# Two waits of TensorE set to earlier counts: the second FFN matmul of superblock 0, and the staging of attention

## The chip, the cores and the metric

The kernel runs on the 8 cores of one Trainium2 chip. Each core holds one of the 8 batch elements and runs the same program; the cores exchange nothing. The metric is the device time in microseconds (us) of the slowest core.

## What is computed

One macaron layer on `x` of shape 8 x 2048 x 1024: half an FFN, attention, half an FFN, each on a LayerNorm of `x`.

```python
x = x + 0.5 * ffn(layernorm(x))
x = x + attn(layernorm(x))
x = x + 0.5 * ffn(layernorm(x))

def ffn(x):   # D = 1024, hidden 4096; two routed experts, one shared
    top1 = argmax(softmax(x @ gate_w.T))
    masked = x[None] * one_hot(top1, 2).T[:, :, None]
    h = relu(einsum('end,edh->enh', masked, w1) + b1[:, None])
    routed = (einsum('enh,ehd->end', h, w2) + b2[:, None]).sum(0)
    return routed + relu(x @ sw1 + sb1) @ sw2 + sb2

def attn(x):  # 16 heads of 64, a plain reshape; q = k = v
    q = x @ wq.T + bq
    qh = q.reshape(16, b, s, 64)
    a = softmax(qh @ qh.T / 32)
    return (a @ qh).reshape(b, s, 1024) @ wu.T + bu
```

## The kernel before

`x` stays in SBUF for the whole kernel (`x_sb`, features on the partitions, 2048 tokens along the free side). The program is written out by hand through a small recorder, `Sched`: `emit` appends an instruction to one engine's list, `bump` raises the recorded count of a semaphore (DVE for VectorE, ACTs for ScalarE, MM for TensorE), and `wait` makes an engine wait until a semaphore has reached a count, unless it has already waited for as much. Each engine runs its list in order, so every wait holds whatever stands behind it on its engine.

**FFN** (`emit_ffn`, run twice). The tokens form four strips of 512. The hidden side of all three experts is cut into 12 superblocks of 1024. For each superblock and strip, `do_mm1` makes the hidden tile in 8 groups of 8 matmuls, into ps_a and ps_b in turn (L556), with ScalarE's Relu after each (L566); `do_mm2` makes the output in 8 groups `dc` of 8 matmuls, into ps_c and ps_d in turn (L593). VectorE adds each group onto `x_sb` (L606 in superblock 0, L613 in the others), and only then is its bank free for the group after next (`ps2_free`). In superblock 0 the LayerNorm is woven in. `sf[st]` makes the sums of a strip (L326, L353). `pf[st]` makes the scale and the mean (TensorE's broadcasts at L391 and L402 among it) and then the normalized strip, in 16 VectorE instructions (L411, L415, eight times each). `gf[st]` makes the gate and masks. The order of superblock 0 is, for each strip: `do_mm1(st)`, `sf[st + 2]`, `pf[st + 1]`, `do_mm2(st)`, where the first two exist for strips up to 1 and 2.

**Attention** (`emit_attn`). 2048 rows are handled in 16 blocks `i` of 128 rows, and each block has 16 rows of tiles `a`. `qproj(half)` makes q for eight blocks, ahead of block 0 and of block 8. `staging(i)` copies a block's q from `q_ap` into `ar_h`, doubled over the partitions, in four groups `b4` of four matmuls (L690) into `stg[b4 % 2]`, which are s0 and s1; VectorE casts each group out (L700). `transposes(i)` follows (L713, cast at L724). `sc_row(i, a)` makes four score matmuls (L742) with ScalarE's exponential after each (L753). Score matmuls go to s0 and s1 in turn, and from `a` = 4 on also to ps_t. `av_row(i, a)` multiplies the exponentials with q, four matmuls (L770). Within a block the order on TensorE is: score rows 0 to 2; AV rows 3 to 15 of the block before; transposes; score rows 3 to 15, with the tail of the block before in between (its sums, L837, L846, and its output projection, L868, L881); AV rows 0 to 2; `staging(i + 1)`. In blocks 0 and 8 the staging and the transposes come straight after `qproj` instead.

The names that the change touches: `xwait_dve` is the VectorE count that the FFN was given as the point from which `x_sb` is complete (0 for the first FFN, attention's last addition for the second). `sch.val(DVE)` is the VectorE count of everything recorded so far. `state["stage_ev"]` and `act_prev` hold the count of the last staging cast; `state["stage_tok"][i]` is what `transposes` and `sc_row` wait for.

Of the kernel before, what the change touches and what calls it, by code (L numbers as in the profile page):

```python
# [29 lines left out]
def c_of_pos(p):  # L30
    return 2 * p if p < 8 else 2 * (p - 8) + 1
# [37 lines left out]
def build(phases=("ffn1", "attn", "ffn2")):  # L69
# [15 lines left out]
    with es:  # L85
# [40 lines left out]
        sch = Sched()  # L126
        X, MM, ACTs, DVE, GP, OUT = "x", "mm", "act", "dve", "gp", "out"
# [14 lines left out]
        def q_ap(kc, t0, w):  # L142
            return ar_b[:, kc * 1024 + t0: kc * 1024 + t0 + w]
# [18 lines left out]
        def w2blk(slot, hc, dc):  # L162
            o = slot * 8192 + hc * 1024 + dc * 128
            return ar_w2[:, o:o + 128]
# [335 lines left out]
        def emit_ffn(xwait_dve, wst, ps_d, ps_w, ps_w2, ps_e, ps_f):  # L500
# [81 lines left out]
            def do_mm2(sup, st, slot, mm2_extra):  # L582
                h_all = max(h_relu_tok)
                for dc in range(NKC):
                    pst = (ps_c, ps_d)[dc % 2]
                    sch.wait("tensor", DVE, max(ps2_free[dc % 2], mm2_extra))
                    if dc > 0:
                        sch.wait("tensor", ACTs, h_all)
                    for hc in range(NKC):
                        if dc == 0:  # L590
                            sch.wait("tensor", ACTs, h_relu_tok[hc])
                        def f2(t, S, _hc=hc, _dc=dc, _slot=slot, _pst=pst):
                            ins = t.matmul(_pst[:, :], w2blk(_slot, _hc, _dc),  # L593
                                           ar_h[:, _hc * TS:(_hc + 1) * TS],
                                           start=(_hc == 0), stop=(_hc == NKC - 1))
                            if _hc == NKC - 1:
                                ins.then_inc(S[MM], 1)
                        sch.emit("tensor", f2)
                    g2 = sch.bump(MM, 1)
                    sch.wait("vector", MM, g2)  # L600
                    sch.wait("vector", DVE, tok_b2)
                    o0 = dc * NT + st * TS
                    if sup == 0:
                        def fx(v, S, _dc=dc, _o0=o0, _pst=pst):
                            xsl = x_sb[:, _o0:_o0 + TS]
                            v.scalar_tensor_tensor(  # L606
                                out=xsl, in0=_pst[:, :],
                                scalar=b2sh[:, _dc:_dc + 1], in1=xsl,
                                op0=ALU.add, op1=ALU.add).then_inc(S[DVE], 1)
                    else:  # L610
                        def fx(v, S, _o0=o0, _pst=pst):
                            xsl = x_sb[:, _o0:_o0 + TS]
                            v.tensor_add(xsl, xsl, _pst[:, :]).then_inc(S[DVE], 1)  # L613
                    sch.emit("vector", fx)
                    stt_tok[dc][st] = sch.bump(DVE, 1)
                    ps2_free[dc % 2] = stt_tok[dc][st]
                    if pending_lnm:
                        pending_lnm.pop(0)()
                while pending_lnm:
                    pending_lnm.pop(0)()  # L620

            sf[0](); sf[1](); pf[0]()
            for st in range(NSTRIP):
                do_mm1(0, st, 0, 0)
                if st + 2 < NSTRIP:
                    sf[st + 2]()
                if st + 1 < NSTRIP:
                    pf[st + 1]()
                do_mm2(0, st, 0, sch.val(DVE))
                if st == 2:  # L630
                    ext["all_ln"] = max(ln_tok)
                if st >= 2:
                    gf[st - 2]()
# [20 lines left out]
        def emit_attn(xwait_dve, s0, s1, d_att, ps_t, ps_rz, hooks):  # L654
# [9 lines left out]
            state = {  # L664
                "exp_tok": {},
                "avtok": {},
                "avfree": 0,
                "stage_tok": {},
                "stage_ev": 0,
                "ufree": 0,  # L670
                "qT_tok": {},
                "zsum_tok": 0,
# [5 lines left out]

            def staging(i, q_ready):
                qoff = (i % 8) * 128  # L680
                act_prev = state["stage_ev"]
                for b4 in range(4):
                    ps = stg[b4 % 2]
                    sch.wait("tensor", ACTs, state["sreg_last"].get(b4 % 2, 0))
                    sch.wait("tensor", DVE, max(q_ready, act_prev))
                    for j in range(4):
                        c = c_of_pos(b4 * 4 + j)
                        hb = (c % 2) * 64
                        def fqq(t, S, _c=c, _hb=hb, _q=qoff, _j=j, _ps=ps):
                            ins = t.matmul(_ps[:, _j * 128:(_j + 1) * 128],  # L690
                                           e2mat[_hb:_hb + 64, :],
                                           q_ap(_c // 2, _q, 128)[_hb:_hb + 64, :],
                                           start=(_j == 0), stop=(_j == 3))
                            if _j == 3:
                                ins.then_inc(S[MM], 1)
                        sch.emit("tensor", fqq)
                    gqq = sch.bump(MM, 1)
                    sch.wait("vector", MM, gqq)
                    def fqqe(v, S, _b4=b4, _ps=ps):
                        v.tensor_copy(ar_h[:, _b4 * TS:(_b4 + 1) * TS],  # L700
                                      _ps[:, :]).then_inc(S[DVE], 1)
                    sch.emit("vector", fqqe)
                    act_prev = sch.bump(DVE, 1)
                state["stage_ev"] = act_prev
                state["stage_tok"][i] = act_prev

            def transposes(i):
                sch.wait("tensor", DVE, state["stage_tok"][i])
# [187 lines left out]
            def qproj(half):  # L896
                t0h = half * 1024
                qev = [0, 0]
                for dc in range(NKC):
                    for st2 in range(2):  # L900
                        t0 = t0h + st2 * TS
                        pst = stg_u[(dc * 2 + st2) % 2]
                        sch.wait("tensor", *wready["wq"])
                        sch.wait("tensor", DVE, max(ln_tok[half * 2 + st2],
                                                    state["avfree"],
                                                    state["ufree"]))
                        sch.wait("tensor", DVE, qev[(dc * 2 + st2) % 2])
                        for kc in range(NKC):
                            def fq(t, S, _kc=kc, _dc=dc, _t0=t0, _pst=pst):
                                ins = t.matmul(_pst[:, :], wqtblk(_kc, _dc),  # L910
                                               ln_ap(_kc, _t0, TS),
                                               start=(_kc == 0), stop=(_kc == NKC - 1))
                                if _kc == NKC - 1:
                                    ins.then_inc(S[MM], 1)
                            sch.emit("tensor", fq)
                        gq = sch.bump(MM, 1)
                        sch.wait("vector", MM, gq)
                        def fqe(v, S, _dc=dc, _toff=t0 - t0h, _pst=pst):
                            v.tensor_scalar_add(q_ap(_dc, _toff, TS), _pst[:, :],
                                                bq_sb[:, _dc:_dc + 1]).then_inc(S[DVE], 1)  # L920
                        sch.emit("vector", fqe)
                        qev[(dc * 2 + st2) % 2] = sch.bump(DVE, 1)
                return max(qev)

            q_ready = qproj(0)
            if "after_qproj0" in hooks:
                hooks["after_qproj0"](sch.val(MM))
            staging(0, q_ready)
            transposes(0)
            for i in range(16):  # L930
                if i == 8:
# [4 lines left out]
                    q_ready = qproj(1)  # L936
# [197 lines left out]
```

## Time and profile before

| | us |
|---|---|
| median of 3 runs | 4235.93 (4235.05 to 4821.63) |
| the profiled execution, own time | 4235.93 |
| its span, slowest core | 4234.3 |
| TensorE busy (matmuls) | 3814.1 |
| ScalarE busy | 1221.5 |
| VectorE busy | 1137.0 |

The span runs from the first to the last instruction of the slowest core, and the execution's own time lies 1.6 us around it. PE stands for TensorE's matmuls, PEld for its weight loads, DVE for VectorE, ACT for ScalarE. A row of a timeline gives the start and the duration in us, and in brackets how long the engine had been idle and what released it. Matmuls are pipelined: a row of 8 starts 8 times, and the next row may start before it ends. PEclk in a row of stretches is the granted clock of TensorE, as a share of its full 2.4 GHz; it takes the two values 0.50 and 1.00, and what lies between is a mean.

### The profile page before, as it was taken

How to read it: one execution, taken by the hardware profiler on the slowest of the kernel's cores; microseconds unless marked ns; L12 is line 12 of the kernel's file. 1: busy time of each engine (PE TensorE's matmuls, PEld its weight loads, DVE VectorE, ACT ScalarE, POOL GpSimd, SP SyncE). 2: the span in 40 equal slices, each digit the busy share in tenths (PEclk: the TensorE clock that was granted, in tenths of full speed). 3: DMA queues.
4: the chain of work that ended last, by engine and by line, in shares of the span. 5: the costliest groups of instructions: out<-in, count | busy, mean ns of one | idle time of the engine just before them, and what ended most of it. 6: DMA issues, size and time to landing. Idle time of an engine off the chain costs nothing. (4 is left out here: it accounts for less than half of the span.)

```text
span 4234.3 us, 45694 instructions; the slowest of 8 cores (4229.7 to 4234.3 us)
## 1 busy us (share of the span) xinstructions
PE 3814.1 (90%) x16880; PEld 1593.2 (38%) x16880; DVE 1137.0 (27%) x2179; ACT 1221.5 (29%) x2956; POOL 48.5 (1%) x67
## 2 busy tenths in 40 slices
PE   3679999999999996888888888867999999999998
PEld 0234444444444431233332333322344444444443
DVE  1332212333222325121231212233222222333222
ACT  1111122111222121765637656421111122111221
POOL 0000000000000000000000000000000000000000
PEclk8799999999999997566575665778999999999999
DMA  7002222222222100100001000210222222222202
GB/s 159 0 1 40 40 40 40 40 40 40 40 40 40 20 1 1 20 1 1 1 1 21 1 1 1 42 18 0 40 40 40 40 40 40 40 40 40 32 10 80
DMA packets 55268, 124.63 MB, mean 29 GB/s; under 512 B 1808, under 2 KB 1808, under 8 KB 53008
## 3 DMA queue, kind: packets, MB, share of 16 engines
q0 software_dynamic: 52144, 104.86, 16.0%
q1 hardware_dynamic: 2912, 16.85, 1.2%
q8 instruction: 144, 2.36, 0.2%
q14 instruction: 68, 0.56, 0.0%
HBM read 218.18 MB, written 8.39 MB: 54 GB/s over the span
## 5 line engine op out<-in xcount | busy, mean ns | idle before, releaser
L566 ACT ACTIVATE ar_h<-ps_a,b1hf 128x512 bf16<-128x512 f32 x384 | 263.9, 687 | 1914.6 <-PE ps_a L556 1914.6
L593 PE MATMUL ps_c<-ar_h,ar_w 128*128 128x512 bf16 x3072 | 735.8, 383 | 78.3 <-DVE ar_ln L415 78.3
L593 PE MATMUL ps_d<-ar_h,ar_w 128*128 128x512 bf16 x3072 | 729.2, 380 | 0.0
L613 DVE TENSOR_TENSOR x_sb<-x_sb,ps_c 128x512 f32<-128x512 f32 x352 | 241.9, 687 | 1501.3 <-PE ps_c L593 1501.3
L556 PE MATMUL ps_a<-ar_b,ar_w 128*128 128x512 bf16 x2048 | 485.8, 379 | 2.8 <-DVE ar_b L522 2.6
L556 PE MATMUL ps_b<-ar_b,ar_w 128*128 128x512 bf16 x2048 | 483.8, 379 | 0.0
L742 PE MATMUL s<-ar_h 64*128 64x512 bf16 x768 | 413.8, 565 | 74.0 <-ACT ar_w L753 53.1
L593 PEld LDWEIGHTS ps_c<-ar_h,ar_w 128*128 128x128 bf16 x3072 | 302.2, 99 | 452.7 <-issue 96.0
L593 PEld LDWEIGHTS ps_d<-ar_h,ar_w 128*128 128x128 bf16 x3072 | 302.0, 98 | 366.8 <-issue 7.8
L566 ACT ACTIVATE ar_h<-ps_b,b1hf 128x512 bf16<-128x512 f32 x384 | 263.9, 687 | 402.5 <-PE ps_b L556 402.5
L753 ACT ACTIVATE ar_w<-s 128x512 bf16<-128x512 f32 x432 | 255.3, 600 | 335.7 <-PE s L742 334.9
L613 DVE TENSOR_TENSOR x_sb<-x_sb,ps_d 128x512 f32<-128x512 f32 x352 | 241.9, 687 | 283.3 <-PE ps_d L593 283.3
L556 PEld LDWEIGHTS ps_a<-ar_b,ar_w 128*128 128x128 bf16 x2048 | 200.1, 98 | 254.4 <-issue 21.8
L556 PEld LDWEIGHTS ps_b<-ar_b,ar_w 128*128 128x128 bf16 x2048 | 200.2, 98 | 234.7
L556 PE MATMUL ps_a<-ar_ln,ar_w 128*128 128x512 bf16 x1024 | 252.0, 387 | 17.8 <-DVE ar_ln L415 17.8
L556 PE MATMUL ps_b<-ar_ln,ar_w 128*128 128x512 bf16 x1024 | 247.5, 385 | 0.0
L522 DVE TENSOR_TENSOR ar_b<-ar_ln,ar_b 128x512 bf16<-128x512 bf16 x512 | 212.9, 418 | 0.0
L742 PEld LDWEIGHTS s<-ar_h 64*128 64x128 bf16 x768 | 75.0, 103 | 361.8 <-issue 360.7
L556 PEld LDWEIGHTS ps_a<-ar_ln,ar_w 128*128 128x128 bf16 x1024 | 101.0, 99 | 151.4 <-issue 35.9
L742 PE MATMUL ps_t<-ar_h 64*128 64x512 bf16 x256 | 147.7, 577 | 5.3 <-ACT p_ex L753 0.4
L556 PEld LDWEIGHTS ps_b<-ar_ln,ar_w 128*128 128x128 bf16 x1024 | 101.7, 99 | 125.1 <-issue 7.8
L753 ACT ACTIVATE ar_ln<-s 128x512 bf16<-128x512 f32 x176 | 105.4, 615 | 43.6 <-PE s L742 43.6
(162 smaller groups left out, 2466.6 us busy)
## 6 DMA issues: line engine op xcount, KB each, us to landing
ar_w<-w1c POOLq DMA_DIRECT2D x24, 2048.0 KB, 18.3
ar_w<-w2c POOLq DMA_DIRECT2D x24, 2048.0 KB, 28.9
x_sb<-x SPq DMA_DIRECT2D x1, 8192.0 KB, 37.3
y<-x_sb SPq DMA_DIRECT2D x8, 1024.0 KB, 10.7
ar_w<-wqt POOLq DMA_DIRECT2D x1, 2048.0 KB, 17.3
ar_w<-wut POOLq DMA_DIRECT2D x1, 2048.0 KB, 16.7
b1hf<-b1h SPq DMA_DIRECT2D x1, 48.0 KB, 38.8
bq_sb<-bqc SPq DMA_DIRECT2D x1, 4.0 KB, 40.1
```

What stands on the lines that cost most here:

```text
L522: v.tensor_mul(lnm_ap(_kc), ln_ap(_kc, _st * TS, TS), mask_ap(_w, _st)).then_inc(S[DVE], 1)
L556: ins = t.matmul(_pst[:, :], w1blk(_slot, _kc, _hc), _rhs(_kc), start=(_kc == 0), stop=(_kc == NKC - 1))
L566: s.activation(ar_h[:, _hc * TS:(_hc + 1) * TS], _pst[:, :], AF.Relu, bias=b1hf[:, _sup * 8 + _hc:_sup * 8 + _hc + 1], scale=0.5).then_inc ...
L593: ins = t.matmul(_pst[:, :], w2blk(_slot, _hc, _dc), ar_h[:, _hc * TS:(_hc + 1) * TS], start=(_hc == 0), stop=(_hc == NKC - 1))
L613: v.tensor_add(xsl, xsl, _pst[:, :]).then_inc(S[DVE], 1)
L742: t.matmul(_sr[:, :], qq_ap(_pa, _h), ar_h[_h:_h + 64, _q4 * TS:(_q4 + 1) * TS], start=True, stop=True).then_inc(S[MM], 1)
L753: s.activation(prow_ap(_a)[:, _q4 * TS:(_q4 + 1) * TS], _sr[:, :], AF.Exp, scale=SCALE, accum_out=_z[:, _a * 4 + _q4:_a * 4 + _q4 + 1]).th ...
```

## The change

Two places are changed, both of them only in what TensorE waits for.

In superblock 0 of each FFN, `do_mm2` gets `xwait_dve` as its extra VectorE count instead of `sch.val(DVE)`. The waits on the bank (`ps2_free`) and on the Relu outputs stay.

In `staging`, one count for the last cast (`stage_ev`, `act_prev`) becomes one count for each of the two banks (`stage_ev2`). A group of staging matmuls waits for the last cast of its own bank instead of the last cast of either. The count that the readers of the staged data wait for is still that of the last cast.

```diff
@@ -626,7 +626,7 @@
                 if st + 1 < NSTRIP:
                     pf[st + 1]()
-                do_mm2(0, st, 0, sch.val(DVE))
+                do_mm2(0, st, 0, xwait_dve)
@@ -666,7 +666,7 @@
-                "stage_ev": 0,
+                "stage_ev2": [0, 0],
@@ -678,11 +678,11 @@
             def staging(i, q_ready):
                 qoff = (i % 8) * 128
-                act_prev = state["stage_ev"]
                 for b4 in range(4):
                     ps = stg[b4 % 2]
                     sch.wait("tensor", ACTs, state["sreg_last"].get(b4 % 2, 0))
-                    sch.wait("tensor", DVE, max(q_ready, act_prev))
+                    sch.wait("tensor", DVE,
+                             max(q_ready, state["stage_ev2"][b4 % 2]))
@@ -700,9 +700,8 @@
                     sch.emit("vector", fqqe)
-                    act_prev = sch.bump(DVE, 1)
-                state["stage_ev"] = act_prev
-                state["stage_tok"][i] = act_prev
+                    state["stage_ev2"][b4 % 2] = sch.bump(DVE, 1)
+                state["stage_tok"][i] = max(state["stage_ev2"])
```

## Rows read from the trace of the kernel before

**Rows 1.** The page: head, part 1, and the TensorE clock of part 2 (tenths, 40 slices).
```profile
span 4234.3 us, 45694 instructions; the slowest of 8 cores (4229.7 to 4234.3 us)
...
PE 3814.1 (90%) x16880; PEld 1593.2 (38%) x16880; DVE 1137.0 (27%) x2179; ACT 1221.5 (29%) x2956; POOL 48.5 (1%) x67
...
PEclk8799999999999997566575665778999999999999
```

**Rows 2.** Waits of TensorE: line <- releaser: us in total, times, longest.
```profile
PE ps_c L593 <- DVE ar_ln L415: 78.3, 6, 13.3
...
PE s L690 <- DVE ar_h L700: 46.7, 48, 1.3
```

**Rows 3.** Timeline, strip 0 of the second FFN: start, us, engine [idle before <-releaser].
```profile
2798.87 0.69 DVE L411 TENSOR_TENSOR ar_ln<-x_sb,ps_f 128x512 bf16<-128x512 f32 x1 [6.03 <-PE ps_f L402]
...
2810.77 0.69 DVE L415 TENSOR_TENSOR ar_ln<-ar_ln,p_ex 128x512 bf16<-128x512 bf16 x1
...
2811.61 3.57 PE L593 MATMUL ps_c<-ar_h,ar_w 128*128 128x512 bf16 x8 [12.98 <-DVE ar_ln L415]
...
2815.30 0.75 DVE L606 SCALAR_TENSOR_TENSOR x_sb<-ps_c,b2sh,x_sb 128x512 f32<-128x512 f32 x1 [3.84 <-PE ps_c L593]
...
2817.40 1.89 PE L593 MATMUL ps_c<-ar_h,ar_w 128*128 128x512 bf16 x8
...
2819.13 1.89 PE L593 MATMUL ps_d<-ar_h,ar_w 128*128 128x512 bf16 x8
```

**Rows 4.** Stretch: busy us of PE, PEld, DVE, ACT, POOL, then PEclk, DMA.
```profile
2811.61:2816.38 4.77, 4.77 (x12) 1.75 (x13) 0.75 (x1) 0.00 (x0) 0.00 (x0) 0.50 0.00 0
```

**Rows 5.** Timeline of one staging, matmuls and casts, to the first score matmuls.
```profile
1802.14 0.60 PE L690 MATMUL s<-ar_b,e2mat 64*128 64x128 bf16 x4
1802.85 0.69 DVE L700 CAST ar_h<-s 128x512 bf16<-128x512 f32 x1 [11.87 <-PE s L690]
...
1803.69 0.38 PE L690 MATMUL s<-ar_b,e2mat 64*128 64x128 bf16 x4 [0.94 <-DVE ar_h L700]
1804.17 0.69 DVE L700 CAST ar_h<-s 128x512 bf16<-128x512 f32 x1 [0.63 <-PE s L690]
...
1807.02 0.69 DVE L700 CAST ar_h<-s 128x512 bf16<-128x512 f32 x1 [0.83 <-PE s L690]
...
1807.86 1.01 PE L742 MATMUL s<-ar_h 64*128 64x512 bf16 x2 [0.94 <-DVE ar_h L700]
```

**Rows 6.** Stretches: three intervals between stagings, then three stagings.
```profile
1738.58:1802.14 63.56, 55.61 (x244) 20.46 (x242) 13.25 (x36) 39.05 (x129) 0.00 (x0) 0.55 0.00 1
1864.16:1925.65 61.49, 53.07 (x244) 19.58 (x242) 13.25 (x36) 38.84 (x129) 0.00 (x0) 0.61 0.00 1
1925.65:1987.00 61.35, 53.30 (x244) 19.64 (x242) 13.25 (x36) 38.84 (x129) 0.00 (x0) 0.61 0.00 1
1738.58:1745.05 6.47, 2.35 (x19) 1.40 (x18) 2.76 (x4) 0.00 (x0) 0.00 (x0) 0.50 0.00 1
...
1864.16:1870.04 5.88, 1.74 (x18) 1.06 (x17) 2.77 (x4) 0.00 (x0) 0.00 (x0) 0.78 0.01 1
1925.65:1931.16 5.51, 1.74 (x19) 1.06 (x18) 2.77 (x4) 0.00 (x0) 0.00 (x0) 0.80 0.00 0
```

**Rows 7.** Timeline of VectorE: two instructions in a row with no wait between.
```profile
1403.61 0.69 DVE L613 TENSOR_TENSOR x_sb<-x_sb,ps_c 128x512 f32<-128x512 f32 x1 [14.52 <-PE ps_c L593]
1404.21 0.42 DVE L522 TENSOR_TENSOR ar_b<-ar_ln,ar_b 128x512 bf16<-128x512 bf16 x1
```

**Rows 8.** Stretches at the AV matmuls of two blocks; the transposes that follow them.
```profile
1878.70:1881.13 2.43, 2.43 (x13) 1.09 (x14) 0.00 (x0) 0.84 (x4) 0.00 (x0) 0.50 0.00 0
1881.13:1891.37 10.24, 8.60 (x73) 3.74 (x69) 1.94 (x5) 4.88 (x17) 0.00 (x0) 1.00 0.00 0
1753.69:1758.25 4.56, 4.56 (x23) 2.02 (x24) 0.00 (x0) 0.86 (x4) 0.00 (x0) 0.50 0.02 4
...
1885.61 0.55 PE L713 MATMUL ps_t<-ident,ar_h 64*128 64x64 bf16 x13
```

## The prediction

> **What bounds the kernel now.** I read the page's head first: all eight cores lie within 4.6 us of each other, so one core stands for the chip. Then its parts 1 and 2: TensorE is busy 90% of the span and is the engine at its limit, and in the middle of the kernel, slices 16 to 26, which hold attention, the clock line of TensorE falls to 5 to 7 tenths of full speed [rows 1]. So a microsecond in which TensorE waits is, as a rule, a microsecond of the span. That leads to the third view, what TensorE waits for [rows 2]. Both edits aim at lines of it: 78.3 us in 6 waits of the second FFN matmul (L593) for the LayerNorm's last multiply (L415), and 46.7 us in 48 waits of the staging matmuls (L690) for their own casts (L700). Together they are 125 us, 3% of the span. How much of it goes is read from the timelines of one place of each kind.
>
> **Edit 1, the wait ahead of `do_mm2` in superblock 0.** The old argument, the VectorE count at the time of the call, holds the first w2 matmul until `pf[st + 1]` has finished all 16 of its VectorE instructions. The new one is a count reached long before. In the timeline those 16 run from 2798.87 to 2811.46 at a pitch of 0.79, and TensorE stands idle for 12.98 us [rows 3]. There are six such places: strips 0, 1 and 2 of both FFNs. Strip 3 calls no `pf`, and its count is met long before, since the view has only six waits of this kind.
>
> The wait does not vanish. The first two groups of eight matmuls (dc 0 and 1) have free banks and can run in the gap. Group 2 needs the bank of group 0 back, and the addition that frees it (L606) stands in VectorE's queue behind the same 16 instructions. So group 2 starts after the last multiply, plus 0.10 to the next VectorE instruction, plus 0.75 for the L606, plus 0.15 to TensorE: 0.85 later than group 0 starts today. Sixteen matmuls are out of the way by then. At full clock a group takes 1.73, the start spacing of later groups, so these are worth 3.45. Gain: 3.45 - 0.85 = 2.6 us.
>
> The clock does not change this much. Today the 16 matmuls run from 2811.61 to 2817.40, in 5.79 us, since the granted clock is 0.50 (the 1.2 GHz level) for the first 4.77 us after the idle stretch [rows 3, 4]. After the edit they run at that level inside the gap, about 6.8 us (16 at the 0.43 of today's cold ones), and TensorE is then idle again for some 7 us, so I expect groups 2 and 3 to pay the same 5.79 - 3.45 = 2.3 us. If the clock stays up over those 7 us, the gain is 2.6 + 2.3 = 4.9. VectorE's and ScalarE's work is unchanged. Nothing else waits behind the removed wait, and the next `do_mm1` follows at once and gives the gain on. Edit 1: 6 x 2.6 = **16 us**, with ends 6 x 2 = 12 (another 0.6 lost in each) and 6 x 4.9 = 29.
>
> **Edit 2, a token per bank in `staging`.** Four groups of four matmuls fill s0 and s1 in turn, and each group is cast by VectorE. Today each group waits for the cast just before it, which read the other bank. The timeline shows the serial chain: cast 0.69, 0.15 to TensorE, group, 0.48 from its start to the next cast, so 1.32 from cast to cast where the group takes 0.38, and some 1.55 where it takes 0.60 and the cast comes 0.71 after its start, as for the first group [rows 5]. From the first staging matmul to the first score matmul this takes 5.51 to 6.47 us [rows 6]; I take 5.6 over the 16 stagings. It is bare: ScalarE, with no exponentials left, shows 0.00 us of work in those stretches [rows 6], so it lies on the path.
>
> After the edit groups 0 and 1 run back to back, and the casts follow one another. VectorE can start an instruction 0.60 after the one before [rows 7]. Cast 2 waits for cast 0's end, 0.15, and 0.48 or 0.71 for the group, so it starts 1.32 to 1.55 after cast 0; cast 3 starts 0.60 to 0.75 after that, and ends 2.6 to 3.0 after cast 0's start. With 0.48 or 0.71 in front and 0.15 behind, the staging takes 3.3 to 3.85; I take 3.4, since most stagings have fast groups. Gain 5.6 - 3.4 = 2.2 us, times 16 = **35 us**. The bounds of each gain are 1.7 (slow groups in a short staging, 5.51 - 3.85) and 3.1. The copied data are the same, and the score rows wait for all four casts as before.
>
> **What is given back through the clock.** From one staging to the next takes about 61.5 us, of which the array has the full clock only for short stretches, 0.61 on the mean [rows 6]. The largest begins in the long run of AV matmuls (L770): these start, and the clock rises 2.43 us later, from 0.50 to 1.00, and stays up 10.24 us [rows 8]. In the first such block it rose 4.56 us after their start, 2.1 later; that interval is 63.56, 2.07 longer than the usual one, and its staging is 0.96 longer than the shortest, which leaves 1.1 us as the price of the late rise [rows 6, 8]. A matmul pair at half clock costs double, so a rise 1 us later costs 0.5.
>
> Further, the intervals hardly follow the staging: stagings of 5.88 and 5.51 stand in intervals of 61.49 and 61.35 [rows 6]. Of 0.37 us only 0.14 shows. So the clock's rises have their own spacing, and AV matmuls that start 2.2 us earlier may have to run longer at the low level. The rise at 2.43 us is the early end of these rows, so a shift costs more often than it gains. I take 0.8 of each 2.2 as lost in the 14 blocks whose staging is followed by another block: **11 us**, from 0 to 14 x 2.2 = 31.
>
> **Sum.** 16 + 35 - 11 = 40 us off the profiled execution, whose own time is 4235.93 around a span of 4234.3, and which is also the median of the runs shown: 4235.9 - 40 = **4196 us**.
>
> The Trainium skill, "TensorE: Matmul & The Clock Gate", section "HAM oscillation — how this bites in real kernels", reports a kernel in which PSUM double-buffering "gave no further gain". Edit 2 is double-buffering of PSUM. By that rule its term would be near 0 and the sum 4220, against 4196 by the rows here; this trace shows no double-buffered staging, so it can't yet say.
>
> **The rivals.**
> - *The clock moves along.* The rises follow the work, and edit 2 keeps all: 4235.9 - 16 - 35 = **4185**. For it: the stretches of full clock begin only in dense array work, which moves with the staging. Against: the 0.14 of 0.37 above.
> - *The staging gain is eaten.* The interval stays at some 61.4 because the AV matmuls wait for nothing but run longer at 1.2 GHz. Only the stagings of blocks 0 and 8 gain, which stand outside the repeating intervals: 2 x 2.2 = 4, less 1 for a clock edge. 4235.9 - 16 - 3 = **4217**. For it: the same 0.14 of 0.37, and the longer first interval. Against: a loss of 2.2 needs a rise 4.4 us later, and the latest seen is 2.1 later than the usual. (The rule named above would land beside this one.)
> - *The clock is better placed.* 47 of 61.5 us are at the low level, so a shift can also win. With the 4.9 in each place of edit 1 and nothing lost in edit 2: 4235.9 - 29 - 35 = **4172**.
> - *Slower: the long high stretch is lost.* If the AV run no longer brought the clock up, its bare part, from 1881.13 to the transposes at 1885.61 [rows 8], would take 4.5 us more in each of 14 blocks: 63 us against 51 gained, **4248**. It decides from a loss of 51 / 14 = 3.6 us a block. Against: the AV matmuls are as dense as before, and the clock rose in every block. Even with all 8.60 us of array work in that stretch doubled, 14 x 8.60 = 120, the time is 4305, short of 2%.
> - *Edit 1 does nothing.* VectorE's queue order stays, so if the two early groups saved nothing the time is 4196 + 16 = **4212**. Against: 16 matmuls do fit in 12.98 us, even at 0.43 each.
>
> **How the numbers follow.** The likeliest, 4196, has 0.45 and its own range 4188 to 4206; full gain 0.22; eaten 0.13; better clock 0.10; edit 1 nothing 0.05; slower 0.05. The range from **4170 to 4217** leaves out the slower case, part of the better clock, and the edge of the eaten case, some 2 in 10. 2% is 85 us, about what a measurement of this kernel can tell from no change; it would need 4151 or less. The best terms together (29 + 35) are 64, so faster by over 2% gets 0.04, slower by over 2% (4321) 0.01, and within 2% gets 0.95.
>
> **What would show each step.** In the changed profile the wait of L593 for L415 is gone, and instead L593 waits for L606, about 7 us in each of six places. The waits of L690 for L700 fall from 48 to 32 at most and from 46.7 to under 15 us, and first staging matmul to first score matmul is near 3.4. The intervals lie between 59.3 and 61.4: near 59.3 the clock moved along, near 61.4 it ate the gain. The prediction is wrong if the casts keep a pitch of 1.3, if the clock rises more than 5 us after the start of the AV matmuls in most blocks, or if the FFN gap shows no matmul.

## The result, and the profile after

| | before | after |
|---|---|---|
| median | 4235.6 us | 4181.6 us |
| span of the slowest core | 4234.3 | 4180.9 |
| wait of L593 for `pf` | 78.3, 6 times | none; for L606 49.9, 6 times |
| wait of L690 for L700 | 46.7, 48 times | 14.0, 31 times |

The change takes 54.0 us off, 1.3%; the ratio is 0.9874, interval 0.986 to 0.9887. The forecast was 4196 us, that is 40 off, with a range of 4170 to 4217. Some executions of every kernel are disturbed and some per cent longer; the ratios leave them out, and every time given here is that of an undisturbed execution or lies among those.

The head, part 1 and the clock line of the page after, to be held against [rows 1]:

```profile
span 4180.9 us, 45678 instructions; the slowest of 8 cores (4176.0 to 4180.9 us)
...
PE 3823.4 (91%) x16880; PEld 1597.4 (38%) x16880; DVE 1133.5 (27%) x2179; ACT 1222.8 (29%) x2956; POOL 48.6 (1%) x67
...
PEclk8899999999999997565575565789999999999999
```

TensorE's busy time is up by 9 us, from 3814.1 to 3823.4, while the span is down by 53. The matmuls are the same 16880, so more of them ran at the low clock. By stage, core 5 of both, the first FFN has 4.4 us more, attention 7.1 (4.9 of them from the first staging to the last), and the second FFN 1.6 less: attention pays some of the gain back.

The same two lines of TensorE's waits as in [rows 2]:

```profile
PE ps_c L593 <- DVE x_sb L606: 49.9, 6, 8.8
...
PE s L690 <- DVE ar_h L700: 14.0, 31, 0.7
```

The timeline at strip 0 of the first FFN, where the order is that of [rows 3]:

```profile
132.04 3.59 PE L593 MATMUL ps_c<-ar_h,ar_w 128*128 128x512 bf16 x8
...
144.26 0.69 DVE L415 TENSOR_TENSOR ar_ln<-ar_ln,p_ex 128x512 bf16<-128x512 bf16 x1
144.87 0.75 DVE L606 SCALAR_TENSOR_TENSOR x_sb<-ps_c,b2sh,x_sb 128x512 f32<-128x512 f32 x1
145.53 0.74 DVE L606 SCALAR_TENSOR_TENSOR x_sb<-ps_d,b2sh,x_sb 128x512 f32<-128x512 f32 x1
...
145.76 3.57 PE L593 MATMUL ps_c<-ar_h,ar_w 128*128 128x512 bf16 x8 [7.57 <-DVE x_sb L606]
...
151.70 1.89 PE L593 MATMUL ps_c<-ar_h,ar_w 128*128 128x512 bf16 x8
```

Groups 0 and 1 now start at 132.04, straight after the matmuls that broadcast scale and mean. The last multiply starts at 144.26, the two additions follow behind it, and group 2 starts at 145.76, 1.50 us after that multiply's start. In [rows 3] group 0 starts 0.84 after it (2810.77 to 2811.61). So 0.66 us go against 3.45 us of matmuls.

The stretch from there on, columns as in [rows 4]: the clock is low again for the first 5.07 us.

```profile
145.76:150.83 5.07, 5.07 (x12) 1.72 (x13) 1.26 (x2) 0.00 (x0) 0.00 (x0) 0.50 0.00 0
```

The timeline of a staging, beside [rows 5]: groups 0 and 1 are one row of 8 matmuls, the casts one row of 4 in 2.61 us, and the score matmuls start at 1789.14, 3.26 us after the first staging matmul (L741 is L742 of the kernel before).

```profile
1785.88 0.62 PE L690 MATMUL s<-ar_b,e2mat 64*128 64x128 bf16 x8
1786.38 2.61 DVE L700 CAST ar_h<-s 128x512 bf16<-128x512 f32 x4 [11.65 <-PE s L690]
...
1787.22 0.38 PE L690 MATMUL s<-ar_b,e2mat 64*128 64x128 bf16 x4 [0.72 <-DVE ar_h L700]
...
1787.82 0.38 PE L690 MATMUL s<-ar_b,e2mat 64*128 64x128 bf16 x4 [0.22 <-DVE ar_h L700]
...
1789.14 0.95 PE L741 MATMUL s<-ar_h 64*128 64x512 bf16 x2 [0.94 <-DVE ar_h L700]
```

Three intervals from staging to staging and two stagings, columns as in [rows 6]:

```profile
1785.88:1846.70 60.82, 54.82 (x244) 20.06 (x242) 13.06 (x36) 38.98 (x129) 0.00 (x0) 0.58 0.00 1
1846.70:1905.47 58.77, 52.47 (x243) 19.72 (x242) 13.13 (x36) 38.84 (x129) 0.00 (x0) 0.62 0.00 1
1905.47:1966.00 60.53, 54.82 (x243) 20.05 (x242) 13.05 (x36) 39.06 (x129) 0.00 (x0) 0.58 0.00 1
1785.88:1789.14 3.26, 1.38 (x18) 0.94 (x17) 2.58 (x4) 0.00 (x0) 0.00 (x0) 1.00 0.00 0
1846.70:1850.20 3.50, 1.62 (x18) 1.19 (x17) 2.65 (x4) 0.00 (x0) 0.00 (x0) 0.92 0.01 2
```

Where it went, both kernels on core 5 (whose span goes from 4231.8 to 4180.9), by the starts of instructions:

| stretch | before | after | saved |
|---|---|---|---|
| start of the kernel to the first w1 matmul | 83.9 | 86.0 | -2.1 |
| from there to the first staging | 1603.5 | 1593.4 | 10.1 |
| first to last staging | 949.1 | 921.7 | 27.4 |
| last staging to the first w1 matmul of the second FFN | 114.8 | 115.1 | -0.3 |
| from there to the end | 1480.4 | 1464.6 | 15.8 |

The first line holds the load of `x` and has no edit in it. The two FFNs give 25.9 us and attention 27.1. The eight cores run the same program and still differ: from first to last staging takes 949.1 or 949.2 us on all of them before, and 919.1 to 924.2 after.

### The profile page after: what moved, and what is told of

The parts are those of the page before. It is cut to its first block and busy times, and to the rows that moved or that the text cites. A ratio compares the mean times of both kernels' runs of the same rounds, so it can differ in the third digit from the quotient of the medians.

```text
span 4180.9 us, 45678 instructions; the slowest of 8 cores (4176.0 to 4180.9 us)
## 1 busy us (share of the span) xinstructions
PE 3823.4 (91%) x16880; PEld 1597.4 (38%) x16880; DVE 1133.5 (27%) x2179; ACT 1222.8 (29%) x2956; POOL 48.6 (1%) x67
## 5 line engine op out<-in xcount | busy, mean ns | idle before, releaser
L593 PE MATMUL ps_c<-ar_h,ar_w 128*128 128x512 bf16 x3072 | 744.9, 386 | 49.9 <-DVE x_sb L606 49.9
L593 PE MATMUL ps_d<-ar_h,ar_w 128*128 128x512 bf16 x3072 | 728.6, 380 | 0.0
L741 PE MATMUL s<-ar_h 64*128 64x512 bf16 x768 | 415.0, 566 | 73.1 <-ACT ar_w L752 51.1
L593 PEld LDWEIGHTS ps_c<-ar_h,ar_w 128*128 128x128 bf16 x3072 | 303.3, 99 | 431.3 <-issue 79.8
L593 PEld LDWEIGHTS ps_d<-ar_h,ar_w 128*128 128x128 bf16 x3072 | 301.8, 98 | 367.9 <-issue 9.4
L741 PEld LDWEIGHTS s<-ar_h 64*128 64x128 bf16 x768 | 74.9, 103 | 361.5 <-issue 361.0
L741 PE MATMUL ps_t<-ar_h 64*128 64x512 bf16 x256 | 151.2, 591 | 4.4 <-ACT p_ex L752 0.4
```

What stands on the lines that cost most here:

```text
L593: ins = t.matmul(_pst[:, :], w2blk(_slot, _hc, _dc), ar_h[:, _hc * TS:(_hc + 1) * TS], start=(_hc == 0), stop=(_hc == NKC - 1))
L741: t.matmul(_sr[:, :], qq_ap(_pa, _h), ar_h[_h:_h + 64, _q4 * TS:(_q4 + 1) * TS], start=True, stop=True).then_inc(S[MM], 1)
```

## The experiments

Nine kernels, each with one thing different from the changed kernel or from before, or two of these put together.

| kernel | time, us |
|---|---|
| `e1_only` | 4210.1 |
| `e2_only` | 4208.2 |
| changed | 4181.6 |
| `dup1`, `dup2` | 4207.4, 4210.0 |
| `bank4` | 4157.7 |
| `weave` | 4168.0 |
| `best` | 4140.5 |
| `early` | 4152.7 |
| `early_bank4` | 4125.9 |

### Each edit alone

`e1_only` is before with this line, and `e2_only` is the changed kernel with it undone:

```diff
-                do_mm2(0, st, 0, sch.val(DVE))
+                do_mm2(0, st, 0, xwait_dve)
```

Expected of `e1_only`:

> Edit 1 alone. In the changed kernel the stretch from the stats of strips 0 and 1 to the next w1 matmul is about 3 us shorter in each of six places (19 us), and the gates after strip 3 are 1.4 and 3.2 us shorter with no edit in them. Theory: all of that follows from edit 1 and adds to edit 2, so this kernel is 23 us faster than before (4212), with attention's intervals as before, 61.3 to 62.4. Rival: only the moved matmuls count, 6 x 2.6 = 16 us (4220), and the gates gain only because attention ends at another moment.

Expected of `e2_only`:

> Edit 2 alone. Theory: stagings shrink by 2.2 us each (36 us in all), of which the intervals from staging to staging keep about 1.65, so that 30 us are left (4206); the 6 waits of L593 for L415 are back at 13 us. Rival: without edit 1 attention starts at another moment and its clock falls differently, so that more is eaten (4220) or nothing (4200).

Measured: 4210.1 us (ratio 0.9942, 0.9925 to 0.996) and 4208.2 us (0.9937, 0.9908 to 0.9966). That is 25.5 and 27.4 less than 4235.6, together 52.9 of the 54.0. TensorE's waits in `e1_only`:

```profile
PE ps_c L593 <- DVE x_sb L606: 50.2, 6, 8.8
...
PE s L690 <- DVE ar_h L700: 46.7, 48, 1.3
```

and in `e2_only`:

```profile
PE ps_c L593 <- DVE ar_ln L415: 78.3, 6, 13.3
...
PE s L690 <- DVE ar_h L700: 14.3, 32, 0.7
```

Each edit takes its own line of the view away and leaves the other as it was; they add. Edit 1 is worth more than the moved matmuls' 16 us also when it is alone, so the 4220 of the rival falls. The other half of that rival, that the gates gain only through the moment at which they come, is taken up behind the experiments.

One thing in it did not fit either theory: attention, where `e1_only` has no edit. On core 4, the slowest, it was slower by 3.7 us than before (952.9 against 949.1 from first to last staging), with 63.7, 62.6, 63.7 and 61.8 us for its second to fifth interval where before has 63.6, 62.0, 61.5 and 61.3. On the other cores of the same execution it took 946.3 us (cores 1, 2 and 5) and 949.1 to 949.4, so the same instructions came out faster than before on some cores and slower on one. The second interval of core 4, then of core 5, columns as in [rows 6]:

```profile
1725.34:1789.05 63.71, 55.75 (x244) 20.53 (x242) 13.25 (x36) 39.04 (x129) 0.00 (x0) 0.55 0.00 1
1726.41:1787.84 61.43, 53.05 (x243) 19.59 (x242) 13.25 (x36) 38.88 (x129) 0.00 (x0) 0.61 0.00 1
```

The difference is in the granted clock, 0.55 against 0.61. From the seventh interval on the two cores agree within 0.1 us.

### Longer stagings: does an interval follow its staging?

The edit, shortened:

```diff
+                for _ in range(1):          # dup2: range(2)
+                    v.wait_ge(S[DVE], base)
+                    v.tensor_copy(ar_h[:, 3*TS:4*TS], stg[1][:, :])   # the last cast, again
                 state["stage_tok"][i] = max(state["stage_ev2"])
```

> The changed kernel with one cast of each staging done twice (the same values again), which makes each staging about 0.8 us longer, 4.2 instead of 3.4. Theory of the clock's own spacing: an interval goes back to the 61.4 us of before at once, because the AV matmuls then start late enough for the clock to rise at the same place of every block; the time is about 4200. Rival, a plain sum: each interval grows by 0.8 to about 60.9, and the time is 4182 + 16 x 0.8 = 4195.

> The changed kernel with one cast of each staging done three times, each staging about 1.6 us longer, 5.0 instead of 3.4. Theory of the clock's own spacing: intervals stay at 61.4, the same as with one extra cast and the same as before the change although the staging is still 0.6 us shorter than before; the time is about 4203. Rival, a plain sum: intervals of 61.7, time 4182 + 16 x 1.6 = 4208, and 0.8 a block more than with one extra cast.

Measured: 4207.4 and 4210.0 us, from one undisturbed execution each. Intervals, stagings and the stretch from the start of the AV matmuls to the rise of the clock in `dup1`:

```profile
1785.13:1846.83 61.70, 54.87 (x244) 20.18 (x242) 13.75 (x37) 39.17 (x129) 0.00 (x0) 0.58 0.00 1
1846.83:1908.05 61.22, 54.68 (x244) 20.05 (x242) 13.75 (x37) 39.17 (x129) 0.00 (x0) 0.58 0.00 1
1785.13:1789.36 4.23, 1.56 (x18) 1.12 (x17) 3.27 (x5) 0.00 (x0) 0.00 (x0) 0.90 0.00 0
1859.60:1864.05 4.45, 4.45 (x23) 2.02 (x24) 0.00 (x0) 0.86 (x4) 0.00 (x0) 0.50 0.00 0
```

and intervals and a staging in `dup2`:

```profile
1789.63:1851.45 61.82, 54.43 (x243) 19.75 (x242) 14.46 (x38) 38.98 (x129) 0.00 (x0) 0.58 0.00 1
1851.45:1912.46 61.01, 53.66 (x243) 20.03 (x242) 14.45 (x38) 38.83 (x129) 0.00 (x0) 0.58 0.00 1
1789.63:1794.49 4.86, 1.39 (x19) 0.95 (x18) 3.96 (x6) 0.00 (x0) 0.00 (x0) 0.84 0.00 0
```

From the changed kernel to `dup1` the stagings grow from 3.4 to 4.2 us on the mean, 12.8 us in all, and first to last staging grows by 20.7 (921.7 to 942.4, core 5): more than they took themselves. The whole kernel is 25.8 us slower, since the second FFN, in which nothing differs, is 7.9 us longer too on this core, and some 3 on most others. The second extra cast (4.2 to 5.0, 12 us in all) costs 3.3 us from first to last staging and 2.6 of the whole kernel. The plain sum wanted 4195 and 4208.

What the two share is the interval: 61.0 to 61.8 us in both, as before with its stagings of 5.5, but for the first two or three intervals of each half: its very first, which has no block before it, takes 47 to 49 us, and behind it up to 63.6 (before) and from 60.5 on (`dup1`) are seen. So over stagings of 4.2 to 5.5 us the interval is 61.4 on the mean whatever the staging takes. The difference is made up in the AV matmuls: in `dup1` they start early and run 4.45 us at the low clock, where before it was 2.43 [rows 8], and the clock then stays up 6.83 us and not 10.24. Of the 23.2 us by which the stagings of `dup1` are shorter than before, 6.7 are left between first and last staging, nearly all of them in the first two intervals of each half. Somewhere between stagings of 4.2 and 3.4 us the interval comes loose: in the changed kernel it is 58.8 to 59.3 in some blocks and 60.5 to 60.8 in others. This is the mechanism that the prediction weighed, and it is now shown: had the edit brought the staging only to 4.2 us, most of its gain would have been lost.

The clock at the AV matmuls of two successive blocks of the changed kernel, beside [rows 8]:

```profile
1797.73:1802.89 5.16, 5.16 (x27) 2.25 (x28) 0.00 (x0) 0.85 (x4) 0.00 (x0) 0.50 0.01 3
1802.89:1809.71 6.82, 5.50 (x53) 2.48 (x50) 1.34 (x4) 2.83 (x10) 0.00 (x0) 1.00 0.00 0
1858.63:1860.91 2.28, 2.28 (x13) 1.06 (x14) 0.00 (x0) 0.86 (x4) 0.00 (x0) 0.50 0.00 0
1860.91:1871.15 10.24, 8.60 (x75) 3.78 (x71) 1.86 (x5) 4.79 (x16) 0.00 (x0) 1.00 0.00 0
```

In the block at 1797.73 the clock rises 5.16 us in and stays up 6.82, and the interval is 60.82. In the next it rises 2.28 us in, stays up 10.24, and the interval is 58.77. Most blocks take the two in turn; in the second half of core 5 two long ones (60.61, 60.70) also follow each other.

### Four banks in the staging

The edit, cut to a few of its lines:

```diff
-            stg = (s0, s1)
+            stg = (s0, s1, ps_rz, ps_t[:, :].bitcast(F32))
-                    ps = stg[b4 % 2]
+                    ps = stg[b4]
...
+                        s.copy(ar_h[:, _b4 * TS:(_b4 + 1) * TS], _ps[:, :])   # odd groups, ScalarE
```

> The changed kernel with the four staging groups in four banks (s0, s1, ps_rz, ps_t), cast in turn by VectorE and ScalarE, so that no group waits for a cast: a staging takes about 2.1 us instead of 3.4. Theory of the clock's own spacing: the AV matmuls then again start early against the rises in every block, intervals come out even, at about 58.0, 2.1 us less than the changed kernel's 60.1 for 1.3 us of staging, and the time is about 4151. Rival, a plain sum: 16 x 1.3 = 21 us, 4161, with intervals of 58.8 that stay uneven.

Measured: 4157.7 us, 24 less than the changed kernel. On core 1, the slowest, two intervals, a staging, and the clock at the AV matmuls of one block:

```profile
1781.50:1839.72 58.22, 52.12 (x243) 19.36 (x241) 11.77 (x34) 40.45 (x131) 0.00 (x0) 0.62 0.00 1
1839.72:1897.55 57.83, 52.16 (x243) 19.34 (x241) 11.77 (x34) 39.99 (x131) 0.00 (x0) 0.62 0.00 1
1781.50:1783.57 2.07, 0.90 (x18) 0.73 (x17) 1.29 (x2) 1.07 (x2) 0.00 (x0) 0.97 0.00 0
1792.02:1795.26 3.24, 3.24 (x17) 1.47 (x18) 0.00 (x0) 0.86 (x4) 0.00 (x0) 0.50 0.02 5
1795.26:1805.50 10.24, 8.39 (x70) 3.60 (x66) 2.23 (x7) 5.27 (x18) 0.00 (x0) 1.00 0.00 0
```

The staging takes 2.07 us, the intervals of the first half are 57.8 to 58.3, and the clock rises 3.1 to 3.3 us into the AV matmuls in every block of that half and stays up 10.24 us in all but its last. In that half stagings that are 1.4 us shorter on the mean (3.4 to 2.1) made the intervals 2.1 us shorter (60.1 to 58.0), as the clock theory wanted and the plain sum (58.8, uneven) did not. Over the whole loop the two are closer: stagings 21.2 us shorter in all, first to last staging 23.6 (921.7 to 898.1). The time is between the two forecasts for two reasons that the trace shows: the second half began with longer intervals, 59.9 and 58.9, before it reached 57.9, and the second FFN, without an edit, takes 3.2 us more on core 1 than on core 5 of the changed kernel (1467.8 against 1464.6). Why the second half began so is open.

### What is left of the FFN gap

`weave` records the normalizing as eight pieces of two instructions, and `do_mm2` lets one go after each of its additions. The line of the call, the rest cut:

```diff
-                    pf[st + 1]()
+                    pf[st + 1](pending_lnm)   # the pieces, two instructions each
```

> The changed kernel with the 16 LayerNorm instructions of pf(st+1) no longer in one block ahead of do_mm2(st), but two of them after each of its additions. Theory: what is left of the FFN gap, some 8 us in each of six places, is VectorE's queue order alone; do_mm2 then runs at VectorE's pace, about 2.3 us a group, 18 us instead of 26, so 6 x 7.5 = 45 us less: 4137. Rival: the next do_mm1 waits for the last normalized tile and takes the gain back, leaving 4165 or more.

Measured: 4168.0 us, 13.6 less and not 45. Waits of the w1 matmuls on the normalized tiles, then the timeline of TensorE at the end of `do_mm2(0)` (L599 is `do_mm2`, L562 `do_mm1` here):

```profile
PE ps_a L562 <- DVE ar_ln L415: 29.1, 22, 3.5
```

```profile
144.01 1.89 PE L599 MATMUL ps_d<-ar_h,ar_w 128*128 128x512 bf16 x8 [0.33 <-DVE x_sb L612]
...
148.51 1.89 PE L599 MATMUL ps_d<-ar_h,ar_w 128*128 128x512 bf16 x7 [0.36 <-DVE x_sb L612]
150.24 1.46 PE L562 MATMUL ps_a<-ar_ln,ar_w 128*128 128x512 bf16 x6
...
154.60 0.58 PE L562 MATMUL ps_a<-ar_ln,ar_w 128*128 128x512 bf16 x1 [1.87 <-DVE ar_ln L415]
154.98 3.34 PE L562 MATMUL ps_b<-ar_ln,ar_w 128*128 128x512 bf16 x8
```

`do_mm2` does run at VectorE's pace: from the sums of strip 2 (L326) to the next w1 matmul it takes 37.3 us instead of 46.2. But 16 normalizing instructions and 8 additions are more VectorE work, about 18.7 us at their pitches, than the 14 us of `do_mm2`, and the last tiles are late for the next stage: `do_mm1(1)` waits 1.87 us for one of them, falls back to the low clock, and takes 18.3 us instead of 13.9. The gates after strip 2 wait in the same way.

By the starts on core 5 the sum is this. Up to the end of `do_mm2(2)` the two FFNs gain 33.5 us; the gates and strip 3 behind it lose 11.7 (40.2 instead of 34.4 in each FFN); and the gates that close superblock 0, with the first w1 matmuls of superblock 1, lose 8.3, because the clock is lower there than in the changed kernel. That leaves 13.5. So the rival of the expectation came out in its number, but waits on late tiles are only a part of what came back.

`early` moves the same work to where VectorE is idle, beside `do_mm1`, which needs only that `pf(2)` and `pf(3)` are recorded one step earlier:

```diff
-                if st + 1 < NSTRIP:
-                    pf[st + 1]()
+                if st == 0:
+                    pf[1]()
                 do_mm2(0, st, 0, xwait_dve)
+                if st + 2 < NSTRIP:
+                    pf[st + 2]()
```

> The changed kernel with pf(2) and pf(3) recorded one step earlier, ahead of do_mm1(1) and do_mm1(2) instead of behind them; their sums are there already. Theory: VectorE's 12.7 us of normalizing then run beside the 14 us of w1 matmuls, and the FFN gap is gone in four of six places without pushing VectorE work onto a later stage (which weaving it between the additions did): 4 x 8.5 us and up to 2 us each of full clock, so 34 to 42 us less: 4144. Rival: as with the weaving, most comes back as waits of the next w1 or gate matmuls, 4165 or more.

Measured: 4152.7 us (ratio to before 0.9791, 0.9728 to 0.9854), 29 less than the changed kernel, where 4144 was expected.

```profile
PE ps_a L556 <- DVE ar_ln L415: 17.8, 16, 1.9
PE ps_c L593 <- DVE x_sb L606: 15.6, 2, 8.0
```

Two of the six waits for L606 are left, those of strip 0, and the w1 matmuls wait as little as before. In the four places the theory holds: by the starts on core 5 both FFNs are 17.6 us shorter up to the end of `do_mm2(2)`, 8.8 a place, although `do_mm1(1)`, which now comes straight after the broadcasts of `pf(2)` and its short idle times, takes 16.1 and 16.5 us instead of 13.9. What is missing to 35 us is again the clock of the closing stretch, in the second FFN: its gates take 26.7 us instead of 23.6, and the first w1 matmuls of superblock 1 16.5 instead of 13.8, together 5.8.

### Together

> Both of these together. If they lie in different stages and add: 4182 - 45 - 31 = 4106. Rival: attention starts at another moment against the clock and keeps less, 4115 to 4125.

> The same together with the four-bank staging, which alone gave 4157.7. Theory: separate stages, they add: 4157.7 - 38 = 4120. Rival: attention starts at another moment against the clock and settles more slowly, 4124 to 4130.

`best` (`weave` with `bank4`) took 4140.5 us (4142.7 in its second undisturbed execution) against the 4106 expected; `weave`'s own shortfall of 31 explains nearly all of it, and 4168.0 + 4157.7 - 4181.6 = 4144 says that the two parts add. `early_bank4` took 4125.9 us, ratio to before 0.9729 (0.9693 to 0.9766), where adding `early` and `bank4` gives 4128.8. It lies in the range of the rival (4124 to 4130), but not for its reason: attention takes what it takes in `bank4` (898.6 against 898.1 us from first to last staging, core 1 of both), and it is `early` that gives 29 us and not the 38 put in. It is the fastest kernel of the study, 110 us under before and 56 under the changed one.

## Why the prediction was right, point by point

- **What bounds the kernel.** Right. 125 us of TensorE's waits were aimed at, 61 of them went (78.3 + 46.7 to 49.9 + 14.0), and the time fell by 54.
- **Edit 1, where the wait goes.** Right in place and order: groups 0 and 1 in the gap, group 2 behind `pf` and one addition. The price of the new order was 0.66 us and not 0.85, because the addition starts 0.61 after the start of the last multiply and not after its end: it does not wait for that multiply's result, and two VectorE instructions overlap as in [rows 7]. The prediction had that row and used it for edit 2 only.
- **Edit 1, the size.** This is the term that was mis-sized: 16 us forecast, 25.9 found in the two FFNs, and 25.5 for `e1_only` as a whole. The six places themselves gave 2.9 to 3.3 us each, 19 in all, by the starts on core 5. The rest lies behind them, where there is no edit: 1.4 and 3.2 us in the gates that close superblock 0 in the first and the second FFN, and 1.3 and 2.8 us in the first w1 matmuls of superblock 1 (16.6 us before, 15.3 and 13.8 after); some 2 us are lost elsewhere. Two stretches of the second FFN, the one of gates, masks and strip 3 that closes superblock 0, and the strip 0 with its gap, before:

```profile
2934.70:2995.90 61.20, 49.31 (x201) 18.88 (x200) 21.77 (x31) 5.50 (x8) 0.00 (x0) 0.91 0.00 1
...
2776.60:2825.20 48.60, 29.94 (x93) 9.74 (x93) 18.92 (x27) 6.40 (x11) 0.00 (x0) 0.75 0.00 0
```

and after:

```profile
2890.20:2948.20 58.00, 46.12 (x202) 18.39 (x201) 21.78 (x31) 5.50 (x8) 0.00 (x0) 0.97 0.00 1
...
2741.70:2787.30 45.60, 31.96 (x94) 10.15 (x94) 18.75 (x27) 6.40 (x11) 0.00 (x0) 0.81 0.00 0
```

  The closing stretch has the same instructions, and takes 58.0 us instead of 61.2 at a mean clock of 0.97 instead of 0.91. In strip 0 the clock is 0.81 instead of 0.75. The prediction let the clock change nothing outside the gap and allowed 2.3 us a place only if it stayed up across it. It did fall across it, as forecast (0.50 for 5.07 us after it). What it left out is that matmuls moved into a gap shift the stages further on against the clock. The 3.2 us are all in the busy time of PE, 49.3 before and 46.1 after, so it is the clock and no wait.

  How much this brings is a matter of the moment. The closing gates take 26.7 to 27.2 us on all eight cores of the kernel before and of `e2_only`, in both FFNs. With edit 1 they take 23.6 to 23.8 in the second FFN of the changed kernel, but 25.4 to 27.1 in its first, by core. `bank4` has the same FFN as the changed kernel, and there the second FFN's gates take 23.6 us on four cores and 25.4 to 25.8 on the other four; core 5, then core 1:

```profile
2896.19:2919.79 23.60, 14.22 (x55) 4.55 (x55) 11.67 (x17) 0.00 (x0) 0.00 (x0) 0.93 0.00 1
2896.53:2921.91 25.38, 16.00 (x56) 4.90 (x55) 11.66 (x17) 0.00 (x0) 0.00 (x0) 0.86 0.00 1
```

  In `early`, which has edit 1 too, all of it is gone in the second FFN:

```profile
2886.46:2913.12 26.66, 17.28 (x55) 5.00 (x55) 11.67 (x17) 0.00 (x0) 0.00 (x0) 0.78 0.00 1
```

  So the 19 us in the six places belong to the edit, and the 8.7 behind them are luck of the moment, which a change further up can take away; without them the time would have been about 4190, an estimate by these numbers. What decides the clock within a closing stretch was not tried and stays open.
- **Edit 2, the staging.** Right: 5.6 to 3.4 forecast, 90.8 / 16 = 5.7 to 54.9 / 16 = 3.4 measured, 36 us in place of 35.
- **The give-back.** Right in mechanism, and shown by `dup1`, `dup2` and `bank4`; 11 us forecast, and 36.0 - 27.1 = 8.9 measured. It is not a constant share of the gain, as "0.8 of each 2.2" had it: down to a staging of 4.2 us it is all of it in the blocks that have settled, and below that first to last staging falls by more than the stagings do (20.7 us for 12.8). The evidence in the prediction (0.14 of 0.37 us) was a sign of the pinned interval and no slope that holds beyond it. The size is good to a few us only, since first to last staging takes 919.1 to 924.2 us by core. The clock rose more than 5 us after the start of the AV matmuls in 4 of 14 blocks on core 5, so the prediction's own sign of being wrong ("in most blocks") did not appear; but some intervals, 58.8 to 59.3, lie under the 59.3 that it had as their lower end.
- **The rival "clock moves along"**, 4185, is nearest in time to the result, but for the wrong reason: intervals were forecast at 59.3 there, and they are 58.8 to 59.3 and 60.5 to 60.8. Its time is met because edit 1's surplus over 16 us (10 us) covers what the clock took (9).
- **The rival "gain eaten"**, 4217, is nearly what `dup1` shows, 0.8 us of staging away: with edit 1 at its real 25.5 us instead of 16 the rival's sum is 4207, and `dup1` took 4207.4. That it meets so closely is chance, since two terms that the rival does not have offset each other: 6.7 us less from first to last staging, and a second FFN that is 3 to 8 us longer than with edit 1 elsewhere.
- **The rival "better placed"**, 4172, needed the clock to stay up across the gap. It fell, and edit 1 came near its 29 us by another way, the stages behind. The 47 of 61.5 us at the low level that it starts from are 48 by the mean of 0.61.
- **The rule on PSUM double-buffering.** `e2_only` is 27.4 us faster than before with nothing but that; the two banks were there already, and one count for both kept them from being used in turn. The Trainium skill's sentence in "TensorE: Matmul & The Clock Gate", section "HAM oscillation — how this bites in real kernels", that it gave no further gain, is of another kernel; the measurement decides here against carrying it over.

## What to carry to other kernels

A token per buffer in place of one for the last use is free, and here it gave 27 of the 36 us that it took out of the serial chain; look for such single tokens wherever two banks alternate. When matmuls are freed from a wait, follow VectorE's queue to see what they wait for next, and ask in which stage VectorE is idle: the same 16 instructions cost 8 us a strip in front of `do_mm2`, came back as new waits when they were woven into it, and cost some 2 us of lower clock, in strip 1 alone, beside `do_mm1`. In a loop that runs mostly at the low clock, a small saving may show as next to nothing or as one and a half times itself, so measure the interval of the loop and the moment at which the clock rises, and do not stop at a saving that shows nothing. Compare the cores as well: where the same instructions take different times on them, a few us of a gain or a loss are the moment's and not the edit's.

## What the runs showed of the hardware

- In attention the clock's rises keep a distance of their own. Blocks whose staging takes 4.2, 4.9 or 5.5 us all repeat at 61.4 us on the mean; at 2.07 us of staging they repeat at 58.0; at 3.3 to 3.5 us some take 58.8 to 59.3 and others 60.5 to 60.8.
- The moment at which a stage meets the clock is worth microseconds with no instruction changed. Attention took 946.3 to 952.9 us on the eight cores of one execution of `e1_only`, and the closing gates of the second FFN 23.6 to 25.8 us on the eight cores of `bank4`. The Trainium skill, "TensorE: Matmul & The Clock Gate", section "What's actually happening", says that the window in which activity is watched is free-running and does not reset when a kernel starts; these differences between cores agree with that.
- Four casts of 128x512 from PSUM, between which VectorE does not wait for itself, took 2.61 us on VectorE together, 0.65 each, where one alone takes 0.69. With a `wait_ge` on VectorE's own count between them the pitch is 0.79, in the normalizing chain and at the extra casts of `dup1` and `dup2` alike.
